# One exponential of 1024 columns per key tile, a ring of three PSUM banks, and self-attention begun a unit earlier

## The reference

```
def attn(x):                                   # 2 heads of 64
    q, k, v = rope(x @ wq.T * s), rope(x @ wk.T * s), x @ wv.T
    return softmax(q @ k.T + causal_mask) @ v @ wo.T
def xattn(x, ctx):                             # 16 heads of 8, 1601 keys
    Q, K, V = x @ Wq + bq, ctx @ Wk + bk, ctx @ Wv + bv
    return softmax(Q @ K.T / sqrt(8)) @ V @ Wo + bo
def ffn(x):                                    # hidden width 512
    even, odd = x[1:17:2], x[2:17:2]           # 8 tokens each
    m1 = (even[:4, :, None] * odd[:4, None, :]).reshape(512, 128)
    m2 = (even[4:, :, None] * odd[4:, None, :]).reshape(128, 512)
    h = gelu(x @ W1.T + scale * x @ m1.T + b1)
    return h @ W2.T + scale * h @ m2.T + b2
x = x + attn(layernorm(x));  x = x + xattn(layernorm(x), ctx);  x = x + ffn(layernorm(x))
```

## Time and profile before

| | us |
|---|---|
| median of 3 runs | 461.98 (461.84 to 470.38) |
| the profiled execution, its own time | 460.36 |
| its span in the profile | 458.6 |
| PE / DVE / ACT / POOL busy in the span | 385.6 / 327.4 / 305.7 / 94.1 |

### The profile page before, as it was taken

One profiled execution on the slowest core, in us unless ns is written; L12 is line 12 of the kernel. 1 busy time (PEld: TensorE's weight loads), 2 busy tenths in 40 slices (PEclk: granted clock), 3 DMA queues, 4 the chain that ended last, 5 costly groups with the idle time before them and its releaser, 6 DMA issues.

```text
span 458.6 us, 9602 instructions
## 1 busy us (share of the span) xinstructions
PE 385.6 (84%) x3632; PEld 180.0 (39%) x3632; DVE 327.4 (71%) x777; ACT 305.7 (67%) x630; POOL 94.1 (21%) x107
## 2 busy tenths in 40 slices
PE   0855879999999889999788989999879999979606
PEld 0535112445443335444335444535335443324205
DVE  2551887978989988798687888797978989910100
ACT  1312014697878777978597778788896899897411
POOL 3530000513100043424000052560000042000050
PEclk9956555999999999999798999999998999997855
DMA  7053470303116220440160321521302310000010
GB/s 251 7 215 95 153 212 39 110 1 109 55 46 168 95 70 16 155 147 18 51 171 2 95 86 36 211 73 41 98 13 76 107 50 1 2 0 1 13 46 11
DMA packets 23387, 36.09 MB, mean 79 GB/s; under 512 B 1654, under 2 KB 20886, under 8 KB 23342
## 3 DMA queue, kind: packets, MB, share of 16 engines
q1 hardware_dynamic: 23342, 35.49, 24.7%
HBM read 19.68 MB, written 11.97 MB: 69 GB/s over the span
## 4 chain that ended last, share of the span: by engine, by line
PE 47%; DVE 27%; ACT 9%; DMA 6%; issue 5%; SPq 2%; POOL 2%; ACTq 0%; DVEq 0%; POOLq 0%
DVE part_max L580 19%; PE wsum L878 14%; PE score L892 10%; PE ring L909 7%; ACT probs L749 4%; PE ring L1039 3%; DMA q_rows<-q_parts 3%; PE ring L999 2%; PE ring L945 2%; PE ring L1031 2%; DMA q_unit<-consts 2%; DVE xn L616 1%; PE ring L934 1%; SPq L399 1%; ACT L749 1%
## 5 line engine op out<-in xcount | busy, mean ns | idle before, releaser
L580 DVE TENSOR_REDUCE part_max<-ring 128x1 f32<-128x401 f32 x512 | 257.8, 566 | 47.1 <-PE ring L909 46.6
L749 ACT ACTIVATE probs<-score 128x512 f32<-128x512 f32 (+1 forms) x416 | 222.7, 597 | 63.5 <-PE score L892 60.2
L909 PE MATMUL ring<-k_unit,q_unit 51*128 51x401 bf16 x512 | 150.0, 359 | 15.7 <-DMA q_unit<-consts 10.9
L878 PE MATMUL wsum<-probs,v_unit 128*32 128x256 f32 (+1 forms) x1664 | 137.0, 398 | 0.5 <-ACT unit_ctx L754 0.2
L892 PE MATMUL score<-q_unit,k_unit 51*128 51x256 bf16 (+1 forms) x832 | 125.2, 279 | 9.2 <-ACT probs L749 8.5
L892 PEld LDWEIGHTS score<-q_unit,k_unit 51*128 51x128 bf16 (+1 forms) x832 | 46.4, 97 | 104.9 <-ACT probs L749 61.6
L909 PEld LDWEIGHTS ring<-k_unit,q_unit 51*128 51x128 bf16 x512 | 47.8, 95 | 45.1 <-DVE part_max L580 27.3
L878 PEld LDWEIGHTS wsum<-probs,v_unit 128*32 128x32 f32 (+1 forms) x1664 | 34.8, 109 | 47.6 <-issue 27.4
L492 POOL TENSOR_TENSOR k_parts<-k_full,c_sb 128x802 bf16<-128x802 f32 x7 | 10.7, 1522 | 174.7 <-ACT k_full L791 174.7
L760 ACT ACTIVATE q_unit<-ring 3x512 bf16<-3x512 bf16 x32 | 18.6, 582 | 24.2 <-PE ring L920 23.9
L720 DVE TENSOR_TENSOR y_out<-ring,x_b 128x256 f32<-128x256 f32 x4 | 1.7, 425 | 35.9 <-PE ring L1039 35.9
(11 more groups left out here) (99 smaller groups left out, 330.2 us busy)
## 6 DMA issues: line engine op xcount, KB each, us to landing
k_unit<-k_rows SPq DMA_DIRECT2D x32, 300.2 KB
v_unit<-v_aug SPq DMA_DIRECT2D x16, 234.0 KB, 6.3
ctx_sb<-ctx_t SPq DMA_DIRECT2D x4, 800.5 KB, 8.9
k_rows<-k_parts SPq DMA_DIRECT2D x4, 601.5 KB, 4.6
k_rows<-k_parts SPq DMA_DIRECT2D x4, 599.2 KB, 3.7
even<-ffn_rows SPq DMA_DIRECT2D x4, 512.0 KB, 4.0
k_rows<-k_parts SPq DMA_DIRECT2D x4, 401.0 KB, 5.0
k_rows<-k_parts SPq DMA_DIRECT2D x4, 399.5 KB, 4.3
```

Of the source, the lines that this page charges most:

```text
L580: v_.tensor_reduce(part_max[:, par, q, head, hp, c:c + 1], ring[s][:, 0:CW], AX.X, ALU.max)\
L749: a_.activation(probs[0:rows, i % PB, :], score[i % EB][0:rows, :], ACT.Exp)\
L878: last = mm(wsum[32 * j:32 * j + 32, 0:S], v_unit[0:rows, u, VQ * t + VW * j:VQ * t + VW * j + 32], probs[0:rows, i % PB, S * (j // 2):S * ...
L909: mm(ring[s][:, 0:CW], q_unit[rows, u, hp, P * q:P * (q + 1)], k_unit[rows, u, L * hp + (CW - 1) * c:L * hp + (CW - 1) * c + CW], start=Tr ...
```

## The change

1. **Scores.** `score` becomes one tensor of four banks, used as two pairs. A tile's scores fill a pair, and ACT takes one exponential of 1024 columns over it. Both banks come free together.
2. **Ring.** `NR` goes from 4 to 3, to pay for the fourth score bank. `probs` has 14 buffers instead of 13.
3. **Side work.** `SIDE` is written anew. `ln1`, `xT`, `qk`, `qks` move to unit 3 of the batch before (and for batch 1 into `START_PLAN`). `h0` and `h1` stand together at (2, 11), `out` at (3, 5) of the next. `split` moves from (2, 5) to (1, 9), which is ahead of both stores; `K3` moves from (1, 1) to (1, 9), `store0` from (1, 4) to (1, 10), `store1` from (1, 12) to (2, 2).
4. **Maxima.** New `AHEAD` and `COUNT`. Six instead of 16 of unit 1's maxima precede the first score, and the first maximum of the next batch's first unit moves from tile (2, 10) to (2, 8).
5. **Self-attention.** The probabilities are normalised before their transposes, by four POOL operations (`pn`), and the product with v is computed transposed, so that `aT` and DVE's scaling go.
6. **Last batch.** The low-rank additions come from PE (`low0`, `low1`, broadcasts of the even tokens) and DVE, not through DRAM and POOL.

```
-EB = 3
-PB = 13
+EB = 4
+PB = 14
-NR = 4
+NR = 3
@@ SIDE, the rows that the prediction speaks of
-    (1, 0): [("prep", "soft")], (1, 1): [("post", "x3T"), ("prep", "K3")], (1, 2): [("prep", "v")],
-    (1, 3): [("prep", "pT0"), ("prep", "pT1")], (1, 4): [("prep", "store0")], (1, 5): [("prep", "av")],
-    (1, 12): [("prep", "store1"), ("prep", "ln2")],
-    (2, 1): [("prep", "x2T")], (2, 3): [("prep", "q")], (2, 4): [("prep", "V0")], (2, 5): [("prep", "split")],
-    (3, 0): [("ctx", 2)], (3, 2): [("post", "h0")], (3, 5): [("post", "h1")], (3, 8): [("post", "out")],
+    (3, 1): [("prep", "ln1", 2)], (3, 4): [("prep", "xT", 2)], (3, 5): [("post", "out", -1)],
+    (3, 7): [("prep", "qk", 2)], (3, 9): [("prep", "qks", 2)],
+    (1, 7): [("prep", "q", 1)], (1, 8): [("prep", "K2", 1)], (1, 9): [("prep", "K3", 1), ("prep", "split", 1)],
+    (1, 10): [("prep", "store0", 1)],
+    (2, 1): [("prep", "V0", 1)], (2, 2): [("prep", "store1", 1)], (2, 3): [("prep", "V1", 1)],
+    (2, 4): [("post", "low", -1)], (2, 5): [("prep", "V2", 1)], (2, 7): [("prep", "V3", 1)],
+    (2, 8): [("prep", "load", 1)], (2, 11): [("post", "h0", -1), ("post", "h1", -1)],
...
-AHEAD = (8, 16, 8, 8)
+AHEAD = (14, 14, 8, 9)
+AHEAD_FIRST = 6
-         (3, 2, 3, 2, 3, 1, 2, 3, 2, 3, 3, 3, 2), (3, 3, 3, 3, 3, 3, 3, 3, 3, 3, 3, 3, 4))
+         (3, 3, 3, 3, 2, 3, 3, 3, 2, 2, 3, 3, 4), (3, 2, 3, 2, 3, 2, 3, 2, 3, 2, 2, 2, 3))
...
@@ POOL
+        elif name == "pn":
+            pool.wait_ge(prsum_done, b + 1)
+            for q in range(QT):
+                cols = slice(0, P) if q == 0 else slice(P, 3 * P)
+                for h in range(HA):
+                    last = g.tensor_scalar(prob_norm[:, h, cols], prob_self[:, h, cols],
+                                           prob_rsum[:, q, h:h + 1], None, ALU.mult)
+            last.then_inc(norm_done, 1)
...
@@ DVE (low1 is alike)
+        elif name == "low0":
+            s, n = take(item)
+            for i in range(4):
+                last = v_.scalar_tensor_tensor(
+                    out=w1_all[:, D * i:D * (i + 1)], in0=ring[s][:, D * i:D * (i + 1)],
+                    scalar=odd_scaled[:, i:i + 1], in1=W("W1")[:, D * i:D * (i + 1)],
+                    op0=ALU.mult, op1=ALU.add)
...
             def exponential(item):
-                act.wait_ge(scores_ready, i + 1)
-                a_.activation(probs[0:rows, i % PB, :], score[i % EB][0:rows, :], ACT.Exp)\
+                act.wait_ge(scores_ready, i + 2)
+                a_.activation(probs[0:rows, i % PB:i % PB + 2, :], score[0:rows, i % EB:i % EB + 2, :], ACT.Exp)\
...
                 if hp == 0 and i >= EB:
-                    pe.wait_ge(probs_done, i - EB + 1)
+                    pe.wait_ge(probs_done, (i - EB) // 2 + 1)
...
@@ PE
+                elif name in ("low0", "low1"):
+                    for i in range(4):
+                        token = 2 * i + 8 * int(name[3]) + 1
+                        last = mm(ring[s][:, D * i:D * (i + 1)], C("ident")[:, token:token + 1].to_broadcast([P, P]),
+                                  xn3[:, 0, :], start=True, stop=True)
```

More of the change, by code:

```diff
@@ L153, in unit_plan @@
     b, u = divmod(v, UB)
-    todo = [("M", v + 1, k) for k in range(AHEAD[(u + 1) % UB], MU)]
-    todo += [("M", v + 2, k) for k in range(AHEAD[(u + 2) % UB])]
-    assert len(todo) == sum(COUNT[u])
+    count = COUNT[u] if v else COUNT_FIRST
+    todo = [("M", v + 1, k) for k in range(ahead(v + 1), MU)] + [("M", v + 2, k) for k in range(ahead(v + 2))]
+    assert len(todo) == sum(count), (v, len(todo), sum(count))
     plan = []
     for t in range(KT):
-        now, todo = todo[:COUNT[u][t]], todo[COUNT[u][t]:]
+        now, todo = todo[:count[t]], todo[count[t]:]
         now = [item for item in now if item[1] < UNITS]
@@ L171, in unit_plan @@
             plan.append(("mT", v + 1))
[L172 to L175, removed]
+        for *what, off in SIDE.get((u, t), []):
+            if 0 <= b + off < B:
+                plan.append((*what, b + off))
         if t >= 2:
@@ L836, in _ @@
             for item in PLAN:
-                if item[0] == "S" and item[4] == 1:
+                if item[0] == "S" and item[3:5] == (1, 1):
                     exponential(item)
@@ L952, in prep @@
                     last.then_inc(filled[s], 1)
-                elif name in ("e0", "e1"):
+                elif name == "e1":
                     pe.wait_ge(qk_done, nb + 1)
-                    h = int(name[1])
-                    rows = slice(DA * h, DA * (h + 1))
-                    s = take(item)
+                    banks = [take(("prep", "e0", nb)), take(item)]
                     for q in range(QT):
-                        last = mm(ring[s][:, P * q:P * (2 * q + 1)], qk_rot[rows, P * q:P * (q + 1)],
-                                  qk_rot[rows, S:S + P * (q + 1)], start=True, stop=True)
-                    last.then_inc(filled[s], 1)
+                        for h in range(HA):
+                            rows = slice(DA * h, DA * (h + 1))
+                            last = mm(ring[banks[h]][:, P * q:P * (2 * q + 1)], qk_rot[rows, P * q:P * (q + 1)],
+                                      qk_rot[rows, S:S + P * (q + 1)], start=True, stop=True)
+                            if q == QT - 1:
+                                last.then_inc(filled[banks[h]], 1)
                 elif name in ("pT0", "pT1"):
-                    pe.wait_ge(soft_done, nb + 1)
+                    pe.wait_ge(norm_done, nb + 1)
                     s = take(item)
                     for i in range(3):
-                        last = turn(ring[s][:, P * i:P * (i + 1)], prob_self[:, int(name[2]), P * i:P * (i + 1)],
+                        last = turn(ring[s][:, P * i:P * (i + 1)], prob_norm[:, int(name[2]), P * i:P * (i + 1)],
                                     C("ident"))
@@ L1026, in post @@
                     turn_tokens(item, xn3)
+                elif name in ("low0", "low1"):
+                    s = take(item)
+                    for i in range(4):
+                        token = 2 * i + 8 * int(name[3]) + 1
+                        last = mm(ring[s][:, D * i:D * (i + 1)], C("ident")[:, token:token + 1].to_broadcast([P, P]),
+                                  xn3[:, 0, :], start=True, stop=True)
+                    last.then_inc(filled[s], 1)
                 elif name in ("h0", "h1"):
-                    pe.wait_ge(low_done, 2 * pb + 1)
-                    s = take(item, ("x3T",))
+                    if pb < B - 1:
+                        pe.wait_ge(low_done, 2 * pb + 1)
+                    s = take(item, ("x3T",) if pb < B - 1 else ("x3T", "low0"))
                     for j in (2 * int(name[1]), 2 * int(name[1]) + 1):
@@ L1034, in post @@
                 elif name == "out":
-                    pe.wait_ge(low_done, 2 * pb + 2)
-                    s = take(item, ("h0", "h1"))
+                    if pb < B - 1:
+                        pe.wait_ge(low_done, 2 * pb + 2)
+                    s = take(item, ("h0", "h1") if pb < B - 1 else ("h0", "h1", "low1"))
                     for q in range(QT):
```

93 lines of the change are left out of this document (51 added, 42 removed), and 4 rows, old and new, of the table SIDE.

## The result

The changed kernel takes **480.94 us** (median of 4 runs, 477.83 to 486.64) against 462.28 for the kernel before in the same rounds: ratio **1.036, interval 1.027 to 1.044**, slower. The forecast was 452 us, in a range of 427 to 472. The profiled execution took 477.83 us for a span of 476.0, which is 17.4 more than the span of before and 27.3 more than the 448.7 of the sum.

The account below looks back on a forecast made before the run. PE's program order was taken as the bound in the middle batches. Start 70.0, batches 97.7, 94.3, 94.3 and 69.5, and tail 22.9 gave a 448.7 us span; with 1.8 and 1.6 added, 452 us, range 427 to 472.

Parts of the forecast that it names:

- Middle without stalls: Unit work of batches 0 to 2, stalls for keys left out: 90.2, 86.8 and 86.8 us.
- Of the idle 7.1 us I keep 3.1: PE's idle time in batch 2: waits for exponentials shrink, waits for the ring of three are new, 3.1 us left.
- rival 2: Ring of three stalls PE in the middle batches: slower, adding 25 us, 477 us in all; chance 0.13.
- PE rarely is three maxima ahead for long: Reason against the ring stalling PE: DVE takes 1.5 us for a tile's three maxima against PE's 1.24.
- late keys: Next batch's first maximum at (2, 8) waits 4.5 us, plus 3.0 for the clock, three times: 22.5 us.
- T: The moment at which PE has filled K3 in tile (1, 9) of batches 0 to 2.
- The half clock behind the wait: After each wait for keys the clock falls to its half level of 1.2 GHz: 3.0 us more.
- Start: Time until the first score: 71.5 becomes 70.0 us, range 68.5 to 72.5, first maximum at 50.3.
- Exponentials: ACT in the middle batches: four of 1024 columns save only four starts over eight of 512; put at nothing.
- Batch 3: Last batch: 73.1 becomes 69.5 us, range 67.5 to 72, as GELU halves leave unit 15 for unit 14.
- Tail: After the last batch: 28.9 becomes 22.9 us, range 21 to 24.3, as eight products replace a 9.50 us wait.
- the returning clock: Tail: a clock coming back gives up to 2.7 us more; half of it taken, 1.4.

Follow-up runs that it names:

- experiment 2: Changed kernel with three single score banks and exponentials of 512 columns, ring kept at three: 483.08 us, ratio 1.050 to the kernel before.
- 1: old_banks: changed kernel with the banks of the kernel before (three single score banks, exponentials of 512 columns, ring of four): 467.46 us, ratio 1.016.
- 4: Kernel before with the new banks alone (two pairs of score banks, exponentials of 1024 columns, ring of three): 481.33 us, ratio 1.046.
- 12: Changed kernel on its own banks, with split at (1, 8) and the next batch's first maximum at (2, 10): 472.1 us, ratio 1.020.
- 9: Mended order, mended_late_maxima: changed kernel, three single score banks, ring of four, split at (1, 8), next first maximum at (2, 10): 450.59 us, 0.966.
- experiment 3: Changed kernel with store0, the first half of the keys, written ahead of the queries' split at (1, 9): 468.78 us, ratio 1.011.
- after: The changed kernel itself, with all parts of the change, against the kernel before: 480.94 us, ratio 1.036.
- experiment 6: Changed kernel with three single score banks, ring of four, and the queries' split one tile earlier, at (1, 8): 460.14 us, ratio 0.982.
- 5: Changed kernel on its own banks with the queries' split one tile earlier, at (1, 8): 472.61 us, ratio 1.020.

## Why the prediction was wrong

**What failed is "Middle without stalls", in its sentence "Of the idle 7.1 us I keep 3.1".** It set the gain of pairs for the exponentials against the new waits for the ring and came out with a gain. In batch 2 PE is idle 16.0 us and not 3.1, of which the wait for keys is 4.8. The runs put the bank alone at 15.6 us (experiment 2 against 1), bank and pairs at 20.5 on the old order (4) and 21.5 on the mended one (12 against 9). The pairs show no worth clear of noise: PE waited for exponentials 8.5 us in all, so there was little to win.

The mechanism stood in the text as rival 2, with 25 us and 477 us for it. That 477 lies so close to 480.94 is in part luck, as it holds 22.5 us for late keys, which cost some 11 (experiment 3). And its banks held "behind a long exponential" aren't needed: with short ones and a ring of three the ratio is 1.050. The mistake is rival 2's chance, 0.13.

The reason given against it, "PE rarely is three maxima ahead for long", looked at DVE's pace (1.5 us for three, PE 1.24). But at that pace the slack between the two is a quarter of a microsecond a tile. Our reading, which the turn of this circle in unit 2 shows once and no run takes apart item by item, is that the fourth bank let PE run past a GELU, a V projection or a turn and still have maxima ready for DVE. The row that hinted at it was on the page of before: 45.1 us of idle time ahead of the maxima's weight loads, 27.3 for DVE, with four banks.

**The late keys were right as a mechanism, wrong as the term that decides.** The prediction gave them 22.5 us; they cost some 11 of after's time. For the keys of batch 1 in after, on SP and then on PE:

```profile
119.66 1.45 SPq L456 DMA_DIRECT2D q_rows<-q_parts  x3
...
124.99 5.16 SPq L449 DMA_DIRECT2D k_rows<-k_parts  x6
134.46 1.47 SPq L403 DMA_DIRECT2D k_unit<-k_rows  x2
```

```profile
116.04 0.94 PE L1033 MATMUL ring<-ctx_sb,w_sb 128*128 128x401 f32 x2
...
143.52 0.51 PE L946 MATMUL ring<-k_unit,q_unit 51*128 51x401 bf16 x1 [3.11 <-DMA k_unit<-k_rows]
```

T is 116.98. Queries done and key writes issued at T + 8.0 (forecast 8.5), keys read from T + 17.5 (17.0), landed by T + 26.5 (24.2: the read takes 9.1 us, not 7.2). PE is there at T + 23.4 and not at 18.0 to 20.3, as the ring holds it up, so it waits 3.1 us; for the next two batches 1.8 and 4.8, together 9.8 in place of 13.5. With four banks PE is there at T + 19.1 and the waits are 15.2 (experiment 6). So one cost hides the other in part. The half clock behind the wait came as said:

```profile
140.40:143.50 3.10, 0.01 (x1) 0.00 (x0) 0.65 (x4) 0.00 (x0) 0.00 (x0) 0.63 0.50 145
143.50:147.00 3.50, 3.48 (x27) 1.09 (x27) 2.10 (x4) 1.55 (x2) 0.00 (x0) 0.50 0.61 190
```

**A piece the prediction did not have** is the split of the queries beside POOL. Moved one tile up, it gives 3.3% with the old banks (1 to 6) and 1.5% with after's (to 5, where the intervals just meet). The move also brings the queries' writes forward in SP's queue, and no run takes the two apart; but the time gained with the old banks lies in units 1, 5 and 9, which end before any wait for keys.

**Start:** 69.9 against 70.0, with the first maximum at 49.97 us against 50.3. **Exponentials** of 1024 columns were put at no gain, and show none clear of noise. **Batch 3:** unit 15 takes 15.3 us, 22.4 before, as the GELU halves with their four table loads have left it; but units 12 to 14 take 58.1 in place of 50.7, and unit 14, into which the halves moved with two loads, has 4.8 of that. With four ring banks units 12 to 14 still take 56.4 (old_banks) to 57.1 (mended_late_maxima). The halves' time was moved and hardly saved: forecast 69.5, measured 73.4.

**Tail:** right in its steps, and 3.4 us too long. PE in the tail of after:

```profile
463.86 0.69 PE L971 MATMUL ring<-c_sb,xn 128*128 128x128 f32 x2 [3.49 <-DVE xn L728]
464.34 3.62 PE L1065 MATMUL ring<-xn,c_sb 128*128 128x128 f32 x16
467.76 2.45 PE L1073 MATMUL ring<-xn_t,w_all 128*128 128x256 f32 x8
471.19 2.02 PE L1082 MATMUL ring<-w_all,hidden 128*128 128x128 f32 x16 [0.98 <-ACT hidden L869]
```

The products for the weights take 3.62 us (4.9 were forecast), with the granted clock at 0.50 all the while. The next start without the 9.50 us of the earlier trace rows and take 2.45 us at a clock of 0.77 (3.78 before), and the output products take 2.02 at 1.00, 3.75 before. So the returning clock gave 3.1 us, and the forecast had taken 1.4. ACT loads the GELU's table beside them, unseen:

```profile
464.99 1.28 ACT L869 ACT_TABLE_LOAD   x1
469.38 1.70 ACT L869 ACTIVATE hidden<-ring,w_sb 128x256 f32<-128x256 f32 x4 [3.11 <-PE ring L1073]
```

**Moving self-attention,** the part with the most lines, gave nothing that shows, though no run has it alone. The mended order has it, the tail and the joined GELU, 0.966; tail and GELU alone are at 0.961.

## What to carry to other kernels

Price a bank by what its shortage costs at the side items, not at the steady tile: before taking one from a ring, read the idle time ahead of the weight loads (PEld) that fill it, and if a good part is already for the draining engine (27.3 of 45.1 us here), expect to pay. Test each part of a bundle alone: here two parts (0.979 and 0.971, 0.961 together) were buried under the rest. When a chain is moved to come "just in time", compute its arrival against the engine at the pace it will have once the other edits work, since one cost can hide another.

## What was not expected of the hardware

DVE instructions of 0.29 and 0.42 us took 1.50 and 1.88 beside POOL's split, while its reductions out of PSUM kept their 0.50. A keys' read of two issues (600 KB) took 8.0 to 9.1 us from issue to landing. And a PE wait of 3.1 us already had the granted clock down to 0.63 in the mean of the wait itself, so that PE resumed at half. In the next batch the clock stayed at 1.00 through a wait of 1.8 us and then had a mean of 0.63 over the 4.6 us behind it.
